# Causal cross attention: the mask products of a batch become a step of their own on TensorE

## The chip, the cores and the metric

The kernel runs on one core of one Trainium2 chip. The time is that of the device, in microseconds (us), from one launch. The kernel before took 1401.39 us (median of 3 runs, 1401.38 to 1406.8).

## The reference

Two decoder layers are computed for `x` of 16 batches x 128 positions x 256 features, each sublayer as `x = x + f(layernorm(x))`: a recurrent mixer, grouped cross attention and a mixture of experts, then windowed self attention, **causal cross attention** and a gated feed-forward. The change is in the causal cross attention alone. What it computes, for each batch:

```
qp = q @ Wq.T                          # q: layernorm(x), 128 x 256;  16 heads of 16 features
k, v = split(latent_kv @ Wkv_expand.T) # latent_kv: 128 x 64
scores = (qh @ kh^T) / sqrt(16)        # per head, 128 x 128
scores = where(tril, scores, finfo.min)
out = softmax(scores) @ vh             # back to 128 x 256
return out @ Wout.T
```

## The kernel before, in words

The kernel is one program of stages, one after the other, each with its own streams for the engines. Stage `cross` handles one batch per step, t = 0 to 15, with two sets of buffers (s = t % 2). `pairs` (line 678) writes steps 0 and 1 out, loops over the pairs of steps 2 to 13, and writes 14 and 15 out. Within an engine the order of instructions is the order of the code; engines meet through semaphores (`wait_ge`; `need` is a wait that is left out where the count is a constant of zero or less).

PSUM has eight banks of 512 columns here. Banks 0 to 3 hold the scores of a batch, one bank per unit u (four heads of 128 columns). Banks 4 and 5 take transpositions, bank 6 the attended values, bank 7 (`PJ`) all projections.

The work of one batch, in the order of its data:

- VectorE normalises the rows (L2851). TensorE turns them (`turn_h`, L2642) and ScalarE copies them out (L2777).
- TensorE projects keys and queries into bank 7 (`project_qk`, L2650 and L2655). ScalarE copies bank 7 to `qk` (L2785).
- GpSimd spreads the keys over a block diagonal of two heads (L2613, two products of 256 columns), and each of the two raises `spread`. After that GpSimd splits pieces of the last stage's weights into a high and a low part (L2625, L2628).
- TensorE projects the values into bank 7 (`project_v`, L2661), once `qk` is copied out. ScalarE copies them (L2789).
- TensorE makes the scores (`scores`). First it writes the additive causal mask into each of the banks 0 to 3, as a product of an identity and the mask in bf16 (L2668, 512 columns, one for each u; 128 rows of the array). Then it adds the products of queries and spread keys (L2673, tiles of 32 rows), eight of them, which the trace counts as 16. A mask product for u must come after VectorE has read that bank for the batch before (`shifted`).
- VectorE takes each row's maximum (L2858) and subtracts it (L2861, which raises `shifted`), for u = 0 to 3. ScalarE takes the exponential (L2794).
- One step later TensorE turns the weights (L2689), ScalarE copies them (L2799), and TensorE multiplies by the values (L2699). ScalarE copies the result (L2804), TensorE turns it (`turn_out`, L2708), and VectorE divides (L2868, L2873). Another step later TensorE turns it again (`turn_out_f`, L2718), ScalarE copies it (L2808), TensorE projects it (L2724), and VectorE adds it to `x` (L2878).

So TensorE's step t (`one`) reads: `scores(t)`, `turn_out_f(t-2)`, `finish_weights(t-1)` with `turn_h(t+1)` in it, `project_qk(t+1)`, `turn_out(t-1)`, `project_v(t+1)`; then `scores(t+1)` begins the next step with its wait for `spread`. The order is written by hand; no planner is involved. VectorE and ScalarE run their own fixed orders, with `shift(t, u)` for u = 0 to 3 first on VectorE. SyncE loads the context of batch t once two batches before it has its values projected (L2597).

The last stage (`silu_ffn`, lines from 2906) starts when the cross stage has ended on all engines.

Of the kernel before, what the change touches and what calls it, by code (L numbers as in the profile page):

```python
# [28 lines left out]
KC = D // P  # L29
# [54 lines left out]
def need(engine, sem, count):  # L84


    if not isinstance(count, int) or count > 0:
        engine.wait_ge(sem, count)  # L88
# [589 lines left out]
def pairs(engine, one, steps=NB):  # L678


    for s in range(2):
        one(s, s, s == 0, False)
    with engine.Fori(1, steps // 2 - 1) as p:
        for s in range(2):
            one(2 * p + s, s, False, False)
    for s in range(2):
        one(steps - 2 + s, s, False, s == 1)
# [1838 lines left out]
def cross(nc, net, sem):  # L2526
# [15 lines left out]
    def number(what, t, u=0):  # L2542

        if what == "h":
            return 0 if isinstance(t, int) and t == 0 else 5 * t - 4
        return 5 * t + 2 + u - (isinstance(t, int) and t == NB - 1)

    def begun(t, n):

        return not (isinstance(t, int) and t < n)  # L2550

    with ExitStack() as ctx:
# [17 lines left out]
        tables_ready = sem("cr_tables")  # L2570
# [7 lines left out]
        spread = sem("cr_spread")  # L2578
# [23 lines left out]
        def _(pool):  # L2602
# [15 lines left out]
            def split_ffn1(t):  # L2618

                piece = bass.ds(t * P, P)  # L2620
                matrices = [[tile.rearrange("p c n -> p (c n)")[:, piece] for tile in of] for of in (
                    (net.gate1_high, net.gate1_low, net.gate1), (net.up1_high, net.up1_low, net.up1),
                    (net.down1_high, net.down1_low, net.down1))]
                for hi, _, w in matrices:
                    own.did(pool.tensor_tensor(hi, w, net.ones[:], ALU.mult))  # L2625
                own.wait()
                for hi, lo, w in matrices:
                    own.did(pool.tensor_tensor(lo, w, hi.bitcast(F32), ALU.subtract))  # L2628
# [5 lines left out]
        def _(pe):  # L2634
            ident = net.const[:, CONST["ident"]]

            def turn_h(t, s):
                pe.wait_ge(normed, t + 1)
                if begun(t, 2):
                    pe.wait_ge(taken, number("p", t - 2, 2) + 1)  # L2640
                for c in range(KC):
                    mm = pe.transpose(ps[:, bank_of("h"), c * P:c * P + P], h_tok[:, s, c * P:c * P + P], ident)  # L2642
                mm.then_inc(turned, 1)

            def project_qk(t, s):
                pe.wait_ge(context_in[s], (t - s) * 8 + 16)
                need(pe, added, t - 2)
                need(pe, proj_taken, 2 * t)
                for oc in range(KC):
                    pe.matmul(ps[:, PJ, D + oc * P:D + oc * P + P], net.xwkv[:, oc * P:oc * P + P],  # L2650
                              context[:, s, :], start=True, stop=True)
                pe.wait_ge(taken, number("h", t) + 1)
                for oc in range(KC):
                    for c in range(KC):
                        mm = pe.matmul(ps[:, PJ, oc * P:oc * P + P], net.xwq[:, c, oc * P:oc * P + P], h_t[:, c, :],  # L2655
                                       start=(c == 0), stop=(c == KC - 1))
                mm.then_inc(projected, 1)

            def project_v(t, s):
                pe.wait_ge(proj_taken, 2 * t + 1)  # L2660
                pe.matmul(ps[:, PJ, 0:D], context[:, s, :], net.xwkv[:, D:2 * D],  # L2661
                          start=True, stop=True).then_inc(projected, 1)

            def scores(t, s):
                pe.wait_ge(spread, KC * (t + 1))
                for u in range(U):
                    need(pe, shifted, U * (t - 1) + u + 1)
                    pe.matmul(ps[:, u, :], ident_b[:], mask.rearrange("p j t -> p (j t)"), start=True, stop=False,  # L2668
                              skip_group_check=True)
                for c in range(KC):  # L2670
                    for u in range(U):
                        g = 32 * u
                        mm = pe.matmul(ps[:, u, c * D:c * D + D], qk[g:g + 32, s, 0, c, :], kbd[g:g + 32, s, c, :, :],  # L2673
                                       start=False, stop=True, skip_group_check=True)
                        if c == KC - 1:
                            mm.then_inc(scored, 1)
# [26 lines left out]
            def turn_out(t):  # L2703
                pe.wait_ge(out_taken, t + 1)

                pe.wait_ge(taken, number("p", t, 3) + 1)
                for u in range(U):
                    mm = pe.transpose(ps[:, bank_of("o"), u * P:u * P + P], out_t[:, u * P:u * P + P], ident)  # L2708
                mm.then_inc(out_turned, 1)

            def turn_out_f(t):
                pe.wait_ge(out_ready, KC * (t + 1))

                pe.wait_ge(proj_taken, 2 * (t + 3) if not (isinstance(t, int) and t >= NB - 2) else 2 * NB)
                if isinstance(t, int) and t >= NB - 2:
                    pe.wait_ge(added, t)
                for c in range(KC):
                    mm = pe.transpose(ps[:, PJ, c * P:c * P + P], out.rearrange("p c u j d -> p c (u j d)")[:, c, :], ident)  # L2718
                mm.then_inc(out_f_turned, 1)
# [7 lines left out]
            def finish_weights(t, s, between=None):  # L2727

                turn_weights(t, s, 0)
                turn_weights(t, s, 1)  # L2730
                if begun(t, 1):
                    project_out(t - 1)
                attend(t, s, 0)
                turn_weights(t, s, 2)
                attend(t, s, 1)
                turn_weights(t, s, 3)
                attend(t, s, 2)
                if between is not None:
                    between()
                attend(t, s, 3)  # L2740

            def one(t, s, first, last):
                scores(t, s)
                if begun(t, 2):
                    turn_out_f(t - 2)
                if first:
                    turn_h(t + 1, 1 - s)
                elif last:
                    finish_weights(t - 1, 1 - s)
                else:  # L2750
                    finish_weights(t - 1, 1 - s, lambda: turn_h(t + 1, 1 - s))
                if not last:
                    project_qk(t + 1, 1 - s)
                if not first:
                    turn_out(t - 1)
                if not last:
                    project_v(t + 1, 1 - s)

            pe.wait_ge(net.in_late, 16 * 6)
            turn_h(0, 0)  # L2760
            project_qk(0, 0)
            project_v(0, 0)
            pe.wait_ge(tables_ready, 2)
            pairs(pe, one)
            t, s = NB - 1, 1
            turn_out_f(t - 1)
# [461 lines left out]
```

## Time and profile before

| | |
|---|---|
| Median of 3 runs | 1401.39 us |
| The profiled execution, its own time | 1413.56 us |
| Span of the profiled execution | 1411.8 us |
| Mean granted clock of TensorE in it | 0.947 of full |
| Busy share of the span: TensorE products, weight loads, VectorE, ScalarE, GpSimd | 87%, 67%, 68%, 54%, 43% |

The span runs from the first to the last instruction. The busy shares are averages over six sublayers that differ; a stage has to be read by itself. The ends of TensorE's instructions are modelled, and neighbours overlap, so distances are best taken from start to start.

### The profile page before, as it was taken

What the parts mean: (1) busy time and instruction counts of PE and PEld (TensorE: products, weight loads), DVE (VectorE), ACT (ScalarE), POOL (GpSimd) and SP (SyncE); (2) the same over time, 40 slices, a digit from 0 to 9 for tenths busy, and PEclk for the clock granted to TensorE, in tenths of its full rate; (3) what the DMA queues carried; (4) which work ended last, traced back from release to release, by engine and by line L of the source; (5) the groups of instructions that cost most, each with busy time, mean ns of one, the idle gap of its engine ahead of it and who ended that gap; (6) DMA issues with size and microseconds to landing.
All of it is one profiled execution on the core that took longest, in us unless ns stands there. A gap on an engine that the chain in (4) does not pass through costs nothing. (4 is left out here: it accounts for less than half of the span.)

```text
span 1411.8 us, 24813 instructions
## 1 busy us (share of the span) xinstructions
PE 1228.2 (87%) x7726; PEld 944.1 (67%) x7726; DVE 958.2 (68%) x1855; ACT 761.3 (54%) x1757; POOL 606.2 (43%) x745
## 2 busy tenths in 40 slices
PE   6894899989989985489999999999977999969998
PEld 4672444478878864367777777777764555648887
DVE  5999899837755358877787778777754666633443
ACT  6442577743545364566666666666643555533332
POOL 2001456452254444776666666666644333320000
PEclk9997899969999998699999999999997999979999
DMA  9001000010035314200000000000000000000000
GB/s 330 1 0 58 10 16 17 9 60 1 23 94 147 98 45 165 108 1 1 2 0 0 0 0 0 0 0 0 1 1 6 3 3 3 2 1 1 15 15 31
DMA packets 27422, 44.74 MB, mean 32 GB/s; under 512 B 5648, under 2 KB 22160, under 8 KB 25936
## 3 DMA queue, kind: packets, MB, share of 16 engines
q1 hardware_dynamic: 23888, 34.31, 7.0%
q0 software_dynamic: 3456, 9.44, 2.5%
q8 instruction: 42, 0.69, 0.2%
q14 instruction: 36, 0.29, 0.1%
HBM read 32.21 MB, written 9.44 MB: 29 GB/s over the span
## 5 line engine op out<-in xcount | busy, mean ns | idle before, releaser
L2334 ACT ACTIVATE wi_weights<-wi_psum,wi_bias,wi_scale 128x128 f32<-128x128 f32 x256 | 113.7, 453 | 120.1 <-DVE wi_bias L2454 120.1
L2109 POOL TENSOR_TENSOR wi_straight<-wi_straight,wi_crossed 128x512 f32<-128x512 f32 x80 | 103.1, 1288 | 10.9 <-DVE wi_crossed L2440 10.8
L978 DVE TENSOR_REDUCE gq_least<-gq_psum 128x4 f32<-128x512 f32 x128 | 84.6, 685 | 15.2 <-PE gq_psum L861 13.5
L2097 POOL TENSOR_TENSOR wi_scratch<-wi_sums,wi_eps 128x4 f32<-128x4 f32 x80 | 33.7, 422 | 129.5 <-DVE wi_sums L2413 128.1
L2098 POOL TENSOR_TENSOR wi_scale<-wi_scratch,minus_half 128x4 f32<-128x4 f32 x80 | 84.6, 1057 | 6.3
L940 ACT ACTIVATE gq_weights_t<-gq_psum 128x512 f32<-128x512 f32 x128 | 67.7, 601 | 23.4 <-PE gq_psum L881 23.2
L2445 DVE TENSOR_REDUCE wi_top<-wi_psum 128x4 f32<-128x512 f32 x64 | 43.8, 685 | 45.8 <-PE wi_psum L2224 45.8
L2175 PEld LDWEIGHTS wi_psum<-const,wi_straight 128*128 128x128 f32 x320 | 39.1, 142 | 53.3 <-issue 34.8
L2858 DVE TENSOR_REDUCE cr_top<-cr_psum 128x4 f32<-128x512 f32 x64 | 43.6, 681 | 45.9 <-PE cr_psum L2673 45.9
L2427 DVE TENSOR_TENSOR wi_straight<-wi_raw,rows 128x512 f32<-128x512 f32 x80 | 71.6, 895 | 0.0
L2233 PE MATMUL wi_psum<-wi_weights_t,wi_values 128*128 128x512 f32 x128 | 68.1, 613 | 2.8 <-DVE wi_weights_t L2461 1.4
L2119 POOL TENSOR_TENSOR wi_weights<-wi_weights,wi_inverse 128x512 f32<-128x512 f32 x64 | 66.4, 1038 | 9.5 <-remote 5.1
L2224 PEld LDWEIGHTS wi_psum<-wi_k_t,wi_q_t 128*128 128x128 f32 x512 | 68.5, 194 | 1.7
L2224 PE MATMUL wi_psum<-wi_k_t,wi_q_t 128*128 128x128 f32 x512 | 68.2, 276 | 0.0
L2613 POOL TENSOR_TENSOR cr_keys_diagonal<-cr_qk,const 128x256 f32<-128x256 f32 x32 | 19.4, 626 | 111.9 <-ACT cr_qk L2785 111.9
L2398 DVE TENSOR_TENSOR wi_out_low<-wi_psum,wi_out_high 128x512 fp32r<-128x512 f32 x64 | 44.0, 687 | 31.7 <-ACT wi_out_high L2341 31.7
L2440 DVE TENSOR_TENSOR wi_crossed<-wi_raw,const 128x256 f32<-128x256 f32 x160 | 65.5, 448 | 0.0
L1247 POOL DMA_INDIRECT ex_slot_rows<-ffn_rows,ex_token x40 | 38.7, 967 | 61.3 <-DVE ex_token L1746 39.4
L2175 PE MATMUL wi_psum<-const,wi_straight 128*128 128x128 f32 x320 | 49.8, 279 | 16.1 <-POOL wi_straight L2109 11.0
L793 POOL TENSOR_TENSOR gq_h_parts<-gq_h_tok,ones 128x512 fp32r<-128x512 f32 x16 | 17.0, 1063 | 108.6 <-DVE gq_h_tok L969 100.7
L3051 DVE TENSOR_TENSOR ff_gated<-ff_gated,ff_psum 128x512 f32<-128x512 f32 x32 | 22.0, 688 | 57.9 <-PE ff_psum L2971 57.6
L861 PE MATMUL gq_psum<-gq_keys_diagonal,gq_h_t 128*128 128x512 f32 x128 | 57.5, 492 | 2.7 <-ACT gq_h_t L930 1.6
(410 smaller groups left out, 3804.5 us busy)
## 6 DMA issues: line engine op xcount, KB each, us to landing
slot_y<-ex_s_out SPq DMA_DIRECT2D x20, 256.0 KB
x<-in_x_dram SPq DMA_DIRECT2D x4, 512.0 KB, 7.9
gate<-in_gate_dram SPq DMA_DIRECT2D x2, 1024.0 KB, 5.6
up<-in_up_dram SPq DMA_DIRECT2D x2, 1024.0 KB, 7.6
down<-in_down_dram SPq DMA_DIRECT2D x2, 1024.0 KB, 9.9
egu<-in_egu_dram SPq DMA_DIRECT2D x1, 2048.0 KB, 14.3
gq_keys_diagonal<-gq_key_parts SPq DMA_DIRECT2D x64, 32.0 KB, 1.9
wo<-in_wo_dram SPq DMA_DIRECT2D x1, 2048.0 KB, 8.8
```

Of the source, the lines that this page charges most:

```text
L861: pe.matmul(ps[:, j % 2, :], h_t[:, n % SLOTS, j * P:j * P + P], kbd[n // 2 % KEYS][:, n % 2, :, :], start=True, stop=True).then_inc(score ...
L940: act.activation(weights_t[:, 4 * (n % 2) + v], ps[:, 2 + v, :], ACT.Exp, scale=-1.0).then_inc(weighed, 1)
L978: dve.tensor_reduce(least[:, n // 2 % 2, n % 2, j, :], ps[:, j % 2, :].rearrange("p (v t) -> p v t", t=P), AX.X, ALU.min).then_inc(topped, 1)
L2098: found = pool.tensor_tensor(scale[:, scale_at], scratch2[:], net.half[:, 0:4], ALU.pow)
L2109: added_up = pool.tensor_tensor(straight[:, at], straight[:, at], crossed[:, at], ALU.add)
L2119: pool.tensor_tensor(weights[:, g % 2], weights[:, g % 2], wide(inverse[:, g % 2], [P, 4, P]), ALU.mult).then_inc(normalised, 1)
L2175: mm = pe.transpose(ps[:, bank_of(what, g), j * P:j * P + P], straight[:, slot(what, g), j, :], ident)
L2224: mm = pe.matmul(bank[:, j * P:j * P + P], q_t[:, g % 2, j, :], k_t[:, s, g, :], start=False, stop=(j == 3), skip_group_check=True)
L2233: pe.matmul(ps[:, AV, :], values[:, s, g * DH:g * DH + DH], weights_t[:, g % 2], start=True, stop=True).then_inc(attended, 1)
L2334: act.activation(weights[:, g % 2, j, :], ps[:, SC + g % 2, j * P:j * P + P], ACT.Exp, bias=bias[:, g % 2, j:j + 1], scale=scale[:, g, j:j ...
L2427: dve.tensor_tensor(straight[:, at], raw[:, at], over_heads(cos[:]), ALU.mult).then_inc(parts, 1)
L2440: dve.tensor_tensor(crossed[:, at, :, to], raw[:, at, :, source], over_heads(sin[:, to]), ALU.mult).then_inc(parts, 1)
```

## The change

The four mask products leave `scores(t)` and become a step `masks(t)`, with their waits for `shifted`. In the step of the batch before, `masks(t + 1)` is called after `turn_out(t - 1)` and ahead of `project_v(t + 1)`. For batch 0 it stands between `project_qk(0)` and `project_v(0)`, and the wait for the two small tables (identity and mask in bf16) moves ahead of it. `scores(t)` keeps the wait for `spread` and the products of queries and keys. No instruction is added or removed, and the order on the other engines stays.

```diff
-            def scores(t, s):
-                pe.wait_ge(spread, KC * (t + 1))
+            def masks(t):
                 for u in range(U):
                     need(pe, shifted, U * (t - 1) + u + 1)
                     pe.matmul(ps[:, u, :], ident_b[:], mask.rearrange("p j t -> p (j t)"), start=True, stop=False,
                               skip_group_check=True)
+
+            def scores(t, s):
+                pe.wait_ge(spread, KC * (t + 1))
                 for c in range(KC):
...
                 if not first:
                     turn_out(t - 1)
                 if not last:
+                    masks(t + 1)
                     project_v(t + 1, 1 - s)
...
             project_qk(0, 0)
+            pe.wait_ge(tables_ready, 2)
+            masks(0)
             project_v(0, 0)
-            pe.wait_ge(tables_ready, 2)
             pairs(pe, one)
```

## Rows read from the trace of the kernel before

**Rows 1.** The table of stretches: busy us of each engine, granted clock, DMA share, GB/s.
```profile
core 0: us, PE busy (x) PEld busy (x) DVE busy (x) ACT busy (x) POOL busy (x), PEclk, DMA share, GB/s
1095.00:1239.00 144.00, 130.00 (x1213) 85.16 (x1212) 92.14 (x180) 83.16 (x167) 48.47 (x104) 1.00 0.01 3
```

**Rows 2.** The waits from 1084 to 1239 us: total us, times, longest.
```profile
POOL cr_keys_diagonal L2613 <- ACT cr_qk L2785: 103.4, 14, 7.7
...
PE cr_psum L2668 <- POOL cr_keys_diagonal L2613: 10.5, 14, 0.8
...
PE cr_psum L2661 <- ACT cr_qk L2785: 4.0, 14, 0.3
```

**Rows 3.** Instructions in order of time, one step: start, us, engine, line, operation.
```profile
1155.52 0.69 DVE L2861 TENSOR_TENSOR cr_weights<-cr_psum,cr_top 128x512 f32<-128x512 f32 x1
...
1156.31 0.60 PE L2708 MATMUL cr_psum<-const,cr_out_t 128*128 128x128 f32 x4
1156.51 0.60 ACT L2785 ACTIVATE cr_qk<-cr_psum 128x512 f32<-128x512 f32 x1 [0.45 <-PE cr_psum L2655]
...
1157.16 0.70 PE L2661 MATMUL cr_psum<-xwkv,cr_context 64*128 64x256 f32 x2 [0.25 <-ACT cr_qk L2785]
...
1157.28 1.18 POOL L2613 TENSOR_TENSOR cr_keys_diagonal<-cr_qk,const 128x256 f32<-128x256 f32 x2 [7.37 <-ACT cr_qk L2785]
...
1158.61 1.03 PE L2668 MATMUL cr_psum<-cr_mask,cr_ident 128*128 128x512 bf16 x4 [0.75 <-POOL cr_keys_diagonal L2613]
...
1159.57 1.15 PE L2673 MATMUL cr_psum<-cr_keys_diagonal,cr_qk 32*128 32x256 f32 x16
...
1160.65 0.46 POOL L2628 TENSOR_TENSOR down_low<-down,down_high  x1
1160.65 0.44 PE L2718 MATMUL cr_psum<-const,cr_out 128*128 128x128 f32 x2
1160.74 0.69 DVE L2858 TENSOR_REDUCE cr_top<-cr_psum 128x4 f32<-128x512 f32 x1 [2.12 <-PE cr_psum L2673]
```

**Rows 4.** Single instructions of that step: the last three transpositions, the last mask.
```profile
1156.42 0.49 PE L2708 MATMUL cr_psum<-const,cr_out_t 128*128 128x128 f32 x3
...
1159.27 0.38 PE L2668 MATMUL cr_psum<-cr_mask,cr_ident 128*128 128x512 bf16 x1
```

**Rows 5.** Durations by line, ns min/median/max: L2661, then the first four of L2673.
```profile
L2661 PE MATMUL cr_psum<-xwkv,cr_context x26: 376/428/480, 1089.9 to 1224.8; 64*128 64x256 f32 x26
...
L2673 PE MATMUL cr_psum<-cr_keys_diagonal,cr_qk x4: 478/478/478, 1159.6 to 1159.6; 32*128 32x256 f32 x4
```

**Rows 6.** Instructions in order of time: the step before the one of rows 3.
```profile
1146.09 1.23 POOL L2613 TENSOR_TENSOR cr_keys_diagonal<-cr_qk,const 128x256 f32<-128x256 f32 x2 [7.41 <-ACT cr_qk L2785]
...
1147.45 1.03 PE L2668 MATMUL cr_psum<-cr_mask,cr_ident 128*128 128x512 bf16 x4 [0.79 <-POOL cr_keys_diagonal L2613]
...
1148.42 1.15 PE L2673 MATMUL cr_psum<-cr_keys_diagonal,cr_qk 32*128 32x256 f32 x16
```

**Rows 7.** TensorE in order of time: batches 0 and 1.
```profile
1066.70 1.22 PE L2661 MATMUL cr_psum<-xwkv,cr_context 64*128 64x256 f32 x2 [0.69 <-ACT cr_qk L2785]
1068.12 1.86 PE L2668 MATMUL cr_psum<-cr_mask,cr_ident 128*128 128x512 bf16 x4 [0.21 <-POOL cr_keys_diagonal L2613]
1069.92 2.09 PE L2673 MATMUL cr_psum<-cr_keys_diagonal,cr_qk 32*128 32x256 f32 x16
...
1075.75 2.08 PE L2655 MATMUL cr_psum<-cr_h_t,xwq 128*128 128x128 f32 x8 [2.64 <-ACT cr_h_t L2777]
1078.51 1.22 PE L2661 MATMUL cr_psum<-xwkv,cr_context 64*128 64x256 f32 x2 [0.69 <-ACT cr_qk L2785]
1079.78 1.89 PE L2668 MATMUL cr_psum<-cr_mask,cr_ident 128*128 128x512 bf16 x4
1081.60 1.53 PE L2673 MATMUL cr_psum<-cr_keys_diagonal,cr_qk 32*128 32x256 f32 x16
```

**Rows 8.** Stretches of the table with a lower clock: cross's start, its end.
```profile
1062.00:1072.00 10.00, 8.91 (x37) 5.21 (x37) 1.53 (x4) 1.36 (x3) 7.82 (x12) 0.50 0.03 9
...
1246.50:1250.00 3.50, 3.41 (x14) 3.08 (x14) 0.04 (x1) 1.58 (x3) 0.00 (x0) 0.55 0.02 5
```

**Rows 9.** Durations, ns min/median/max: VectorE's normalisation, all 16.
```profile
L2851 DVE TENSOR_SCALAR cr_h_tok<-x,mean_var,rstd x16: 403/435/1007, 1061.6 to 1224.9; 128x256 f32 x12, 128x256 f32<-128x256 f32 x4
```

**Rows 10.** Groups by line, windowed stage: busy us, mean ns, idle before.
```profile
L2398 DVE TENSOR_TENSOR wi_out_low<-wi_psum,wi_out_high 128x512 fp32r<-128x512 f32 x64 | 44.0, 687 | 31.7 <-ACT wi_out_high L2341 31.7
```

## The prediction

> **What bounds the kernel now.** I read the page's shares first. They are averages over unlike stages, so the next view is the table of stretches for the cross stage alone. There TensorE is busy 130.0 of 144 us, at full clock, and no other engine is above 92.1 [rows 1]. TensorE sets the pace of the stage, and what it loses in each step are waits. The view of waits names two that matter: 10.5 us for the spread keys, in front of the masks, and 4.0 us for the copied `qk`, in front of the values' projection. Each comes 14 times, once per batch [rows 2]. GpSimd's own 103.4 us of waiting [rows 2] shows that it is not short of time: it sits until `qk` arrives.
>
> One step in order of time shows why [rows 3]. The projection of keys and queries ends. ScalarE copies `qk` (1156.51 to 1157.11), GpSimd spreads the keys (1157.28 to 1158.46), and the masks start at 1158.61, 0.15 after it. Beside that chain of about 2.2 us TensorE has only the four transpositions (from 1156.31) and the values' projection (from 1157.16). It then spends 1158.61 to 1159.57 on masks, which need neither `qk` nor the keys. Only at 1159.57 come the products that do. VectorE waits until 1160.74, so it and everything behind it follow the scores.
>
> **The change, part by part.** Nothing is removed or added; four products per batch change place on one queue.
>
> *Masks out of the way of the scores.* From the first mask to the first score is 1159.57 - 1158.61 = 0.96 us [rows 3], and 1148.42 - 1147.45 = 0.97 in the step before [rows 6]; the steps alternate between these two forms. If the scores may start where the masks start now, each batch gains 0.96.
>
> *Do they fit into the gap?* I lay out the new order from start to start. The last transposition starts at 1156.42 + 0.49 - 0.27 = 1156.64: three of them last 0.49 and one 0.27 (0.49 less two steps of 0.11) [rows 4]. The masks start at 1156.75. They stream every 0.22, and from the last mask (1159.27) to the first score (1159.57) is 0.30 [rows 3, 4]; so a group of masks and the change to tiles of fewer rows take 0.96 together. The values' projection then starts at 1157.71. `qk` was copied out at 1157.11, so its wait is gone. Its two products: the first lasts up to 480 ns after a stop, the other 376 [rows 5]; with 0.70 for both, the second starts 0.70 - 0.376 = 0.32 later. It streams 0.22, and I allow 0.09 for the change of tile as at the masks: scores could start at 1157.71 + 0.32 + 0.31 = 1158.34. The keys let them start at 1158.61. TensorE has 0.27 to spare, so the keys decide. In the other form (transpositions from 1145.04, same layout, keys 0.13 before 1147.45) the spare is about 0.38 [rows 6].
>
> *First score after a stop.* Now the first four score products stand behind the masks and still last 478 ns against 374 for the rest, so they already pay for an exposed weight load [rows 5]. I charge nothing more. What the trace doesn't show is a score group right behind a 64-row product. From below it costs no more than the change from the masks (0.08, in my layout); from above I take that the scores start only when the modelled end of the projection has passed, 1157.71 + 0.70 = 1158.41, still 0.20 inside. I take the former; neither touches the sum at full clock.
>
> The Trainium skill, TensorEngine Tiling (Array Packing), section Tiling Modes, says that changing the tiling mode drains TensorE. The row agrees in kind: 0.30 against 0.22 from the last mask. Here the changes per batch go from three (to 64 rows, back to 128, to 32) to two (to 64, to 32); by that rule with a full drain behind each the sum would be 0.2 us smaller, all of it in batches 0 and 1.
>
> *The moved wait for `shifted`.* The masks of t+1 now wait, early, for VectorE's subtraction of u = 3 of batch t, and behind them in the queue stand the projection, ScalarE's copy of the values, and the scores. That subtraction ends at 1155.52 + 0.69 = 1156.21; the masks come at 1156.75, 0.54 later [rows 3]. Both hang on the scores' start, so the cover stays when the step shrinks. Past it and the spare of 0.27, each us of a late VectorE costs one us. I cost it at nothing.
>
> *What is later.* The projection of values starts about 0.55 later (1157.71 for 1157.16). ScalarE copies it after its exponential of u = 3, then waits for bank 7 at 1161.12 less 0.96; the copy (0.38) ends near 1158.8. SyncE's next context load slips by as much, and its context is used more than a step later. GpSimd's weight splitting ends at 1161.11 [rows 3], and now runs beside VectorE's first maximum and subtraction, which start near 1159.78. The nearest row for that is L2398 of the windowed stage, the same shape from PSUM and SBUF: 687 ns in the mean [rows 10], against 0.69 here; no cost. From above, VectorE's normalisation, which does fall beside GpSimd's work, goes from 403 to 1007 ns [rows 9]; I keep that for the rival.
>
> *Batches 2 to 15:* 14 x 0.96 = 13.5 us.
>
> *Batches 0 and 1* run at the 1.2 GHz level (granted 0.50) [rows 8]. There masks take 1069.92 - 1068.12 = 1.80 and the projection up to 1.27 (1078.51 to 1079.78, with no wait behind it), so TensorE and not the keys decides, and the gain is the idle time that is filled. In batch 1 the projection of queries ends at 1077.83 and streams on some 0.18 before its modelled end, so the next product could start at 1077.65; the values start at 1078.51 [rows 7]. That is 0.86, less 0.08 for one change of tile that was hidden in the wait: 0.8. Batch 0 has the same and 0.15 held by the keys (1.42 from projection to masks against 1.27) [rows 7]: 0.9. The bounds are the rows' idle times (0.69 + 0.69 + 0.21 = 1.6) and half a mask group each more (3.4). I take 1.7.
>
> **Sum:** 13.5 + 1.7 = 15.2 us. Profiled execution: 1413.56 - 15.2 = 1398.4. It was 12.2 us above the median of the runs, which I put down to nothing in this stage. Median: 1401.4 - 15.2 = 1386.2. All of it passes to the end, because the last stage starts when this one has ended.
>
> **The rivals.**
>
> *The clock moves (0.15).* TensorE is busier from 1066 to 1082, so its clock may rise earlier. At full clock the scores of batch 0 take 1.15 instead of 2.09 and the masks of batch 1 1.03 instead of 1.89 [rows 3, 7]: 1.8 us more, 1384.4. The reverse is a lower clock in other stretches near the stage's end: one such stretch holds 3.4 us of work at 0.55 [rows 8], and another like it costs about 1.6, 1387.8. For it speaks only that these stretches move against the rest.
>
> *TensorE becomes the bound before the scores (0.09).* If the unseen change from 64 to 32 rows costs 0.3 us more than the spare, the gain is 0.66 x 14 + 1.7 = 10.9 and the time 1390.5. Against it: changes of tile cost 0.08 where a row shows them [rows 4].
>
> *The gain goes nowhere (0.05).* If the scores were held by something after the keys, the time stays at 1401.4. Against it: the masks start 0.15 after GpSimd ends, and the score products follow without a stop [rows 3].
>
> *The early wait holds the queue: slower (0.02).* Place: the masks' wait for u = 3. If GpSimd's splitting stretches VectorE's first maximum and subtraction as it did the normalisation (x 2.5), `shifted` is 0.69 x 1.5 x 2 = 2.06 late. Less 0.54 cover and 0.27 spare that is 1.25 per batch against 0.96 gained: 14 x 0.29 = 4.1, less 1.7, so 1403.8. It decides from a delay of 0.54 + 0.27 + 0.96 = 1.77. Rows 10 speak against it.
>
> **How the numbers follow.** The forecast (1385 to 1388) has 0.69. The range takes in the clock case and the TensorE-bound one and the bounds of the first two batches: 1383 to 1391.5. A measurement of this kernel can tell about 0.5%, 7 us, from no change. Faster by more than that is under 1394.4: the first three cases, 0.93. Within it: 0.06, the cases of no gain and nearly all of the slower one. Slower: 0.01.
>
> **What would show it.** Right: in a step at full clock the order is L2708, L2668, L2661, L2673, the scores' idle time is 0.2 to 0.4 us until L2613, no wait stands in front of L2661 or L2668, and a step is 10.25 us where it was 11.2. Wrong: a wait of L2668 for L2861; no wait of L2673 for L2613 (TensorE bounds); L2858 or L2861 longer than 0.7 beside GpSimd; a step that shrank by less than 0.9; or batches 0 and 1 off their 1.7 because the clock rose at another time.

## The result: medians of 1401.64 and 1384.72 us, a ratio of 0.9864, more gained than forecast

| | before | after |
|---|---|---|
| Median (4 runs each) | 1401.64 us (1401.38 to 1406.8) | 1384.72 us (1384.03 to 1385.64) |
| Ratio, 95% interval | | 0.9864 (0.9843 to 0.9886) |
| Span of the profiled execution | 1411.8 us | 1382.5 us |
| Cross stage, start of the first transposition to start of the last addition to `x` | 196.3 us | 178.4 us |

The medians differ by 16.9 us, and the ratio says 19 us (16 to 22); forecast were 15.2. The median of after lies inside the forecast range, 0.9864 of the time before (1382.6) just below its lower end of 1383. The two profiled executions differ by 29.3 us, but 11.9 of these lie ahead of the cross stage, where nothing was changed: its first transposition starts at 1062.2 in the one and at 1050.3 in the other.

In the changed kernel the mask products are L2667, the scores L2675, and lines behind them are 2 or 4 higher. One step, in order of time (start, us, engine, line, operation), beside [rows 3]:

```profile
1136.09 0.69 DVE L2865 TENSOR_TENSOR cr_weights<-cr_psum,cr_top 128x512 f32<-128x512 f32 x1
...
1136.89 0.60 PE L2710 MATMUL cr_psum<-const,cr_out_t 128*128 128x128 f32 x4
1137.09 0.60 ACT L2789 ACTIVATE cr_qk<-cr_psum 128x512 f32<-128x512 f32 x1 [0.45 <-PE cr_psum L2655]
1137.22 0.64 PEld L2667 LDWEIGHTS cr_psum<-cr_mask,cr_ident 128*128 128x128 bf16 x4
...
1137.54 0.81 PE L2667 MATMUL cr_psum<-cr_mask,cr_ident 128*128 128x512 bf16 x3
...
1137.86 1.18 POOL L2613 TENSOR_TENSOR cr_keys_diagonal<-cr_qk,const 128x256 f32<-128x256 f32 x2 [6.32 <-ACT cr_qk L2789]
...
1138.28 0.70 PE L2661 MATMUL cr_psum<-xwkv,cr_context 64*128 64x256 f32 x2
...
1139.09 0.74 PEld L2675 LDWEIGHTS cr_psum<-cr_keys_diagonal,cr_qk 32*128 32x128 f32 x16 [0.52 <-POOL cr_keys_diagonal L2613]
1139.09 1.15 PE L2675 MATMUL cr_psum<-cr_keys_diagonal,cr_qk 32*128 32x256 f32 x16
...
1140.26 0.69 DVE L2862 TENSOR_REDUCE cr_top<-cr_psum 128x4 f32<-128x512 f32 x1 [1.07 <-PE cr_psum L2675]
```

The order is the forecast one: transpositions (L2710), masks (L2667), values (L2661), scores (L2675). (The record of the first mask product is missing; its weight load is there.) From the transpositions to the scores it took 1159.57 - 1156.31 = 3.26 us [rows 3] and takes 1139.09 - 1136.89 = 2.20. The projection of values no longer waits, the masks wait for nothing (the subtraction ends at 1136.78, some 0.5 ahead of them), and the scores start 0.05 after GpSimd ends at 1139.04. In the table of stretches the steady part now reads, beside [rows 1]:

```profile
1079.00:1209.00 130.00, 126.59 (x1198) 85.33 (x1204) 93.04 (x180) 83.51 (x168) 46.98 (x101) 1.00 0.01 3
```

TensorE is busy 97% of it, where it was 90%. In the waits from 1085 to 1200 us, the ones in front of TensorE's values and masks are gone, and this is left in front of the scores:

```profile
PEld cr_psum L2675 <- POOL cr_keys_diagonal L2613: 6.5, 11, 0.6
...
PE cr_psum L2675 <- POOL cr_keys_diagonal L2613: 1.5, 6, 0.2
```

### The profile page after: what moved, and what is told of

Same layout as the page of the kernel before. It is cut to its first block and busy times, and to the rows that moved or that the text cites. A ratio compares the mean times of both kernels' runs of the same rounds, so it can differ in the third digit from the quotient of the medians.

```text
span 1382.5 us, 24786 instructions
## 1 busy us (share of the span) xinstructions
PE 1214.4 (88%) x7679; PEld 940.9 (68%) x7726; DVE 957.8 (69%) x1855; ACT 760.1 (55%) x1757; POOL 606.2 (44%) x745
## 5 line engine op out<-in xcount | busy, mean ns | idle before, releaser
L2224 PEld LDWEIGHTS wi_psum<-wi_k_t,wi_q_t 128*128 128x128 f32 x512 | 68.4, 194 | 1.7
```

The costliest lines, as they stand in the source:

```text
L2224: mm = pe.matmul(bank[:, j * P:j * P + P], q_t[:, g % 2, j, :], k_t[:, s, g, :], start=False, stop=(j == 3), skip_group_check=True)
```

## The experiments

Two theories have to be kept apart. A: the place of the masks on TensorE's queue gives a fixed amount per batch, as long as the keys and not TensorE set the start of the scores. B: the rest of the difference between the first two traces is TensorE's clock, which falls to its 1.2 GHz level in other places in every execution. C came up while the traces were read: a wait whose count is held in a register costs time when it stands behind the wait that matters.

All traces, cut at the start of the scores of batches 0, 1, 2 and 15 (s0, s1, s2, s15), in us. The stage goes from the start of its first transposition to the start of its last addition to `x`:

```
                      stage  to s0  s0-s1  s1-s2  s2-s15 (a batch)  after s15   stage starts at
before                196.3  7.72   11.68  10.70  145.42 (11.186)   20.75       1062.2
e5  before            196.3  7.72   11.69  10.71  145.44 (11.188)   20.75       1050.5
e10 before            196.4  7.72   11.61  10.86  145.42 (11.186)   20.75       1050.4
e12 before            196.3  7.69   11.56  10.92  145.42 (11.186)   20.75       1050.0
after                 178.4  6.44   10.69  10.66  131.94 (10.149)   18.63       1050.3
e1  after             179.1  6.49   10.69   9.26  131.94 (10.149)   20.68       1050.2
e11 after             179.1  6.60   10.54   9.26  131.94 (10.149)   20.75       1055.3
e2  waits hoisted     195.0  7.72   11.74  10.64  144.71 (11.131)   20.21       1051.0
e3  split wait        175.8  6.60   10.60   9.07  128.79 ( 9.907)   20.76       1052.5
e4  values first      183.2  7.53   11.50  10.09  134.80 (10.369)   19.32       1049.2
e6  one extra mask    175.4  6.84    8.00   9.29  132.23 (10.172)   19.09       1049.8
e7  four extra masks  186.9  7.65    9.97   9.93  139.98 (10.768)   19.32       1050.8
e8  masks too early   208.1  6.60   13.26  11.74  156.57 (12.044)   19.95       1050.2
e9  split and extra   179.3  6.94   10.79   9.29  131.57 (10.121)   20.73       1049.4
```

The column from s2 to s15 repeats to 0.02 us in four traces of the kernel before and to 0.01 in three of the changed one. It is the yardstick for everything that follows.

**The changed kernel again (e1, 5 runs; e11, one run).** No edit.

> The changed kernel again, to have a second trace of it. Theory A (place of the masks): scores to scores takes 10.15 us a batch from batch 2 to 15, as in the first trace (11.19 before), and this is the same in every execution; the gain over the kernel before is 13.5 us there and about 2.3 in batches 0 and 1. Theory B (clock): the parts of the cross stage that the first trace shows beyond this (2.1 us less after the last scores, 1.0 us more between the scores of batches 1 and 2) are stretches at the 1.2 GHz level that fall elsewhere by chance; they differ in this trace by up to 2 us. Rival: they come from the order and repeat to 0.2 us. Time: 1384 to 1386 us.

> The changed kernel, a third trace. 10.15 us a batch. Theory B: the time between the scores of batches 1 and 2 (10.66 and 9.26 so far) and after the last scores (18.65 and 20.66) fall again among such values, with no fixed pair.

Measured for e1: 1384.5 us (1380.26 to 1387.03), ratio 0.9854 (0.9828 to 0.988); for e11: 1389.62 in one run. The step is 10.149 us in both, as in the first trace. The parts around it move: s1 to s2 took 10.66, 9.26 and 9.26 us in the three traces, and the time after s15 18.63, 20.68 and 20.75. The rows say that it is the clock. After s15, in the first trace of the changed kernel:

```profile
1218.93 0.44 PE L2720 MATMUL cr_psum<-const,cr_out 128*128 128x128 f32 x2 [0.87 <-DVE cr_out L2877]
1219.20 1.04 PE L2691 MATMUL cr_psum<-const,cr_weights 128*128 128x128 f32 x8
1220.08 1.03 PE L2726 MATMUL cr_psum<-xwout,cr_out_f 128*128 128x256 f32 x4
```

and in e1:

```profile
1217.42 0.61 PE L2720 MATMUL cr_psum<-const,cr_out 128*128 128x128 f32 x2 [0.87 <-DVE cr_out L2877]
1217.82 1.91 PE L2691 MATMUL cr_psum<-const,cr_weights 128*128 128x128 f32 x8
1219.53 1.74 PE L2726 MATMUL cr_psum<-xwout,cr_out_f 128*128 128x256 f32 x4
```

The same instructions of the same program, with the same waits ahead of them, last 1.04 and 1.91 us. For these stretches of the changed kernel B holds.

**The kernel before again (e5, 12 runs; e10 and e12, one run each).** No edit.

> The kernel before again, for a second trace of it. Theory B (clock): the 12 us by which its first profiled execution was above the median lie ahead of the cross stage and are not there again, and the stretches at the 1.2 GHz level at the end of the cross stage (2.1 us more than in the changed kernel) and after batch 1 differ from its first trace. Rival: both repeat. Scores to scores 11.19 us a batch in any case. Time 1401.4 us.

> The kernel before, a third trace. The steps from scores to scores are 11.19 us a batch. Theory B (clock by chance): the time after the last scores (20.8 and 20.7 us in two traces, 18.7 and 20.7 in two of the changed kernel) or the one between the scores of batches 1 and 2 is off by 1 to 2 us in some of the three traces of each kernel, and so is some stage ahead of the cross stage in an execution near 1407. Rival: the kernel before always has 20.7 to 20.8 after the last scores.

> The kernel before, a fourth trace, for the same question: 11.19 us a batch, and the 5.5 us between its two groups of times (near 1401.5 and near 1407) lie ahead of the cross stage, not in it. Rival: they lie in the cross stage.

Measured: e5 1402.48 us (1401.31 to 1407.46), e10 1401.93, e12 1401.41. The 11.9 us ahead of the stage were not there again. They arose between 290 and 500 us, in the mixture of experts: the first trace is 1.3 us ahead of e5's when it enters this stretch and 12.1 us behind it at the end. The granted clock from 290 to 400 us and from 400 to 500 was 0.87 and 0.95 there, and 0.91 and 1.00 in e5. An estimate from these shares gives the clock at most 110 x 0.04 + 100 x 0.05, some 9 of the 13.4 us. So B holds for a part of this difference only, and no cause is shown for the rest. The stage itself took the same in both.

The time after s15 was 20.75 in all four traces of the kernel before: B's expectation that it would vary there too missed, and the rival to it holds. That stretch was at the low clock in every trace of the kernel before, and in two of three of the changed one. s1 to s2 moved by 0.2 only.

The times of the kernel before fall into two groups. Of 50 runs (the first 4, 34 measured beside e1 to e8, and e5's 12), 24 lie between 1400.8 and 1402.7 and 23 between 1406.0 and 1407.7. None of the traces fell on one near 1407, so e12's question, where in the program the difference lies, has no answer from the kernel before itself. That it goes with the clock can be read from the runs: in the 46 of them whose mean granted clock is on record, it is 0.948 to 0.952 in the lower group and 0.946 or 0.947 in the upper. The span times one less this mean is the most that the lower level can have cost. It comes to 70.8 and 75.4 us in the mean of the two groups, 4.6 of the 5.2 us between them. For the changed kernel, e11 at 1389.62 us (clock 0.945) started its cross stage at 1055.3, 5.1 us later than e1 at 1384.5 (clock 0.949), and the stage itself took the same: that difference lies ahead of the stage.

**The waits alone, in the kernel before (e2, 12 runs).** The masks stay behind the wait for the keys.

```diff
             def scores(t, s):
+                need(pe, shifted, U * t)
                 pe.wait_ge(spread, KC * (t + 1))
                 for u in range(U):
-                    need(pe, shifted, U * (t - 1) + u + 1)
                     pe.matmul(ps[:, u, :], ident_b[:], ...
```

> The kernel before, with the masks where they were, behind the wait for spread keys; only the four waits for the subtractions of the batch before (counts held in registers inside the loop) are one wait now and stand ahead of the wait for the keys. Theory C: in the kernel before, the evaluation of these counts stands between the end of GpSimd's spreading and the first mask (0.13 and 0.15 us there, 0.05 before the first score in the changed kernel). Then the first mask starts 0.05 us after GpSimd ends, each of the 14 looped and late batches gains 0.08 to 0.10 us, 1.2 us in all, 1400.2 us. Rival: the 0.1 us belongs to a bf16 mask product after a stop; then nothing changes: 1401.4 us and still 0.13 to 0.15.

Measured: 1403.42 us (1399.75 to 1409.8), where 1400.2 was expected; ratio 0.9992 (0.9974 to 1.0009). The time can't resolve an effect of this size; the trace can. In the kernel before, within the loop and then in the written-out step 15 (GpSimd's spreading, then the first weight load of the masks):

```profile
1157.28 1.18 POOL L2613 TENSOR_TENSOR cr_keys_diagonal<-cr_qk,const 128x256 f32<-128x256 f32 x2 [7.37 <-ACT cr_qk L2785]
...
1158.60 0.55 PEld L2668 LDWEIGHTS cr_psum<-cr_mask,cr_ident 128*128 128x128 bf16 x4 [1.15 <-issue]
...
1235.51 1.18 POOL L2613 TENSOR_TENSOR cr_keys_diagonal<-cr_qk,const 128x256 f32<-128x256 f32 x2 [7.12 <-ACT cr_qk L2785]
...
1236.74 0.55 PEld L2668 LDWEIGHTS cr_psum<-cr_mask,cr_ident 128*128 128x128 bf16 x4 [0.97 <-POOL cr_keys_diagonal L2613]
```

and in e2, within the loop:

```profile
1145.73 1.18 POOL L2613 TENSOR_TENSOR cr_keys_diagonal<-cr_qk,const 128x256 f32<-128x256 f32 x2 [7.29 <-ACT cr_qk L2785]
...
1146.96 0.55 PEld L2668 LDWEIGHTS cr_psum<-cr_mask,cr_ident 128*128 128x128 bf16 x4 [1.07 <-POOL cr_keys_diagonal L2613]
```

From GpSimd's end to the weight load it is 0.14 us in the loop of the kernel before, where the counts of the waits in between are held in registers, 0.05 in its step 15, where they are constants, and 0.05 in e2's loop, where they stand ahead. The releaser changes too: "issue" in the first, GpSimd in the other two. The rival as it was put (a bf16 product after a stop, so that nothing changes) falls. But e2's steps 14 and 15, which are written out, went the other way, though no count is in a register there. Step 15 in e2:

```profile
1223.56 1.18 POOL L2613 TENSOR_TENSOR cr_keys_diagonal<-cr_qk,const 128x256 f32<-128x256 f32 x2 [7.18 <-ACT cr_qk L2785]
...
1224.86 0.56 PEld L2668 LDWEIGHTS cr_psum<-cr_mask,cr_ident 128*128 128x128 bf16 x4 [1.03 <-issue]
```

GpSimd ends at 1224.74, and the weight load comes 0.11 later instead of 0.05. It is 0.12 for batch 0 in both traces too, where the wait for the keys is the only one in front of the masks. So with constants the gap is 0.05 when another, long met, wait stands behind the one for the keys, and 0.11 or 0.12 when none does. The scores of the changed kernel, fp32 products with the keys' wait alone in front of them, start 0.05 after GpSimd in the loop and in steps 14 and 15, so the product may matter too. Which waits stand where changes the gap by up to 0.09 us; that the register is the cause is not shown, and e2 also made one wait of four.

With this the step closes. In the loop the two forms of the step fell from 11.27 and 11.16 to 11.20 and 11.07 us, and the last two steps rose by 0.08 each: 11 x 0.08 - 2 x 0.08 = 0.72 us less over the 13 batches, or 0.055 in the mean, as in the table.

**Masks behind the values (e4, 6 runs).** Half of the change: ahead of the wait for the keys, but not filling the time in which ScalarE copies.

```diff
-                    masks(t + 1)
                     project_v(t + 1, 1 - s)
+                    masks(t + 1)
...
-            masks(0)
             project_v(0, 0)
+            masks(0)
```

> The changed kernel with the masks behind the projection of values, still ahead of the wait for the keys. This undoes half of the change. Theory A: the projection waits for the copied queries and keys again (0.25 to 0.33 us), the masks then end 0.2 to 0.25 us after the keys are there, so TensorE bounds: 10.35 to 10.4 us a batch against 10.15, 3 us in 14 batches, and 0.8 us more in each of batches 0 and 1: 1389 us. Rival: only being ahead of the wait for the keys counts, the order within does not: 1384.7 us.

Measured: 1388.94 us (1387.25 to 1395.77), ratio 0.9912 (0.9886 to 0.9937), 10.369 us a batch. Both are what A expects. In its trace the values wait again, GpSimd is done at 1140.34, and the scores start 0.29 later, because TensorE is still at the masks:

```profile
1139.04 0.70 PE L2661 MATMUL cr_psum<-xwkv,cr_context 64*128 64x256 f32 x2 [0.25 <-ACT cr_qk L2789]
1139.16 1.18 POOL L2613 TENSOR_TENSOR cr_keys_diagonal<-cr_qk,const 128x256 f32<-128x256 f32 x2 [6.50 <-ACT cr_qk L2789]
...
1139.89 0.81 PE L2667 MATMUL cr_psum<-cr_mask,cr_ident 128*128 128x512 bf16 x3 [0.16 <-issue]
1140.63 1.15 PE L2675 MATMUL cr_psum<-cr_keys_diagonal,cr_qk 32*128 32x256 f32 x16
```

So of 1.04 us a batch, 0.82 come from being ahead of the wait for the keys and 0.22 from being ahead of the values.

**The spare time, filled (e6, 5 runs; e7, 6 runs).** One, or all four, of the mask products of a batch issued twice; `start=True` makes the second write the same.

```diff
-                    pe.matmul(ps[:, u, :], ident_b[:], mask...
+                    for _ in range(2 if u < 1 else 1):      # e7: u < 4
+                        pe.matmul(ps[:, u, :], ident_b[:], mask...
```

> The changed kernel with the first mask product of each batch issued twice: 0.22 us more TensorE work per batch at the full clock, 0.43 at the lower one. Theory A: in the changed kernel the keys bound the scores and TensorE has 0.2 to 0.35 us to spare, so from batch 2 on this is hidden but for at most 0.04 us a batch; batches 0 and 1 pay 0.43 each: 0.9 to 1.4 us in all, 1385.6 to 1386.1 us. Rival (TensorE bounds): 14 x 0.22 + 0.9 = 4 us, 1388.7 us.

> The changed kernel with every mask product issued twice: 0.86 us more per batch at the full clock. Theory A: the spare is used up and the rest shows, 0.86 less 0.2 to 0.35 is 0.5 to 0.65 us a batch, 7 to 9 us in 14 batches, and 1.7 in each of batches 0 and 1: 1395 to 1397 us. Rival: no spare, 12 + 3.4 us, 1400 us.

Measured: e6 1385.71 us (1380.47 to 1388.19), 10.172 a batch: 0.22 us of work costs 0.023. e7 1394.21 us (1392.53 to 1399.49), 10.768 a batch: 0.86 costs 0.62, so 0.24 were free. Its step is as A expects, its time 0.8 us under the expected range. The changed kernel has about 0.24 us of TensorE time to spare per batch in the mean, and the keys set its pace.

**The wait for the keys split (e3, 5 runs; e9, one run).** If the keys bound, letting the first half of the scores start on the first half of the keys should free that spare.

```diff
             def scores(t, s):
-                pe.wait_ge(spread, KC * (t + 1))
                 for c in range(KC):
+                    pe.wait_ge(spread, KC * t + c + 1)
```

> The changed kernel, where the scores of the first half (c = 0) wait for the first of GpSimd's two spreading products alone, and those of the second half for the second. Theory A, with the keys as the bound of the changed kernel and TensorE 0.2 to 0.35 us behind: scores start that much earlier, 0.2 to 0.3 us a batch, 2.5 to 4 us in all: 1381 to 1382.5 us. Rival 1: TensorE itself was the bound: no change, 1384.7. Rival 2: the second wait between the products costs 0.1 us or more a batch: 1383 or above.

> The kernel with the split wait for the keys, and the first mask product of each batch issued twice, one look. Theory A: with the wait split TensorE itself is the bound (9.91 us a batch), so the 0.22 us that was all but free in the changed kernel (10.15 to 10.17) now shows in full: 10.1 to 10.15 us a batch. Rival: 9.93, the product is still hidden and the keys or another engine set the pace.

Measured: e3 1382.09 us (1378.45 to 1383.47), ratio 0.9835 (0.9813 to 0.9857), 9.907 a batch, 0.24 less than the changed kernel. It beats both kernels in the trace; by the times its interval overlaps e1's. In e3 TensorE is busy 118.87 of 120 us:

```profile
1137.25 1.18 POOL L2613 TENSOR_TENSOR cr_keys_diagonal<-cr_qk,const 128x256 f32<-128x256 f32 x2 [6.00 <-ACT cr_qk L2789]
1137.67 0.70 PE L2661 MATMUL cr_psum<-xwkv,cr_context 64*128 64x256 f32 x2
...
1138.29 1.15 PE L2675 MATMUL cr_psum<-cr_keys_diagonal,cr_qk 32*128 32x256 f32 x16
```

The scores start 0.62 after the values, 0.14 before GpSimd is done with the second half. e9 adds e6's extra product to it, and now 0.22 us of work cost 10.121 - 9.907 = 0.21. The same product is free in one kernel and paid in full in the other: with the split wait, TensorE bounds.

**Masks earlier still (e8, 6 runs).** The forecast's slower rival, made to happen by the place of the masks and not, as there, by a slower VectorE.

```diff
                 if not last:
+                    masks(t + 1)
                     project_qk(t + 1, 1 - s)
...
-                    masks(t + 1)
                     project_v(t + 1, 1 - s)
```

> The changed kernel with the masks of the next batch ahead of the projection of keys and queries. The fourth mask then has to wait for VectorE's last subtraction (7.8 us after the start of the scores, where that projection starts 6.25 after it), and the projection stands behind it. Theory A: the projection starts at 8.15 instead of 6.25, and nothing fills the gap behind it: 12.0 us a batch, where the kernel before has 11.2 and the changed one 10.15; slower than before by 10 us: 1408 to 1412 us. Rival (the early wait costs nothing, because the subtraction is in time): 11.1 us a batch, 1400 us.

Measured: 1414.18 us (1412.75 to 1417.66), ratio 1.0074 (1.0051 to 1.0097), 12.044 a batch: slower than the kernel before. The time is 2 us above the expected range (s0 to s1 took 13.26), and the step is as expected.

```profile
1161.41 0.69 DVE L2865 TENSOR_TENSOR cr_weights<-cr_psum,cr_top 128x512 f32<-128x512 f32 x1
1162.16 0.39 PE L2667 MATMUL cr_psum<-cr_mask,cr_ident 128*128 128x512 bf16 x1 [0.79 <-DVE cr_weights L2865]
1162.48 0.71 PE L2650 MATMUL cr_psum<-cr_context,xwkv 64*128 64x128 f32 x4
...
1165.16 1.23 POOL L2613 TENSOR_TENSOR cr_keys_diagonal<-cr_qk,const 128x256 f32<-128x256 f32 x2 [8.27 <-ACT cr_qk L2789]
1166.45 1.15 PE L2675 MATMUL cr_psum<-cr_keys_diagonal,cr_qk 32*128 32x256 f32 x16 [0.71 <-POOL cr_keys_diagonal L2613]
```

The fourth mask waits 0.79 us for the subtraction that ends at 1162.10, the projection of keys stands behind it, and the gap that the masks used to fill is idle again.

## Why the mechanism was right, and which steps of the sum failed

Two terms of the sum were too small. "Batches 2 to 15: 14 x 0.96" measured 1.037 a batch, and the 1.7 us for batches 0 and 1 measured 2.1 to 2.3. With them the sum is 16.8 us where it was 15.2, and the traces show 17.2 to 18.0 us for the stage. A third step failed in a smaller way: the clock was left out of the sum, as a rival with 0.15. The paragraphs below take these one by one, after what was right.

**What bounds, and the mechanism: right.** The scores followed the masks, which waited for something they did not need. The signs came: the order, no wait in front of values or masks, and the scores waiting for GpSimd. Their idle time was put at 0.2 to 0.4 us and is 0.12 and 0.24 in the two forms of the step. The step shrank to 10.15, forecast 10.25.

**Fit into the gap: right.** The layout put the values 0.96 behind the first mask and the scores, were the keys there, 0.63 behind the values. The values start 1.39 behind the transpositions (forecast 1.40), and e3, where the keys don't hold them, starts its scores 0.62 behind the values. In the changed kernel they start 0.81 and 0.94 behind them, so the spare is 0.19 and 0.32. It was put at 0.27 and 0.38, and e7 measured 0.24 in the mean.

**The drain between tiling modes: too strong here.** Scores behind the values start 0.62 later in e3, before the modelled end of the projection at 0.70; in batch 1 of the changed kernel, at the lower clock, they start 1.15 behind (1066.30 to 1067.45), modelled end 1.22. What the Trainium skill, TensorEngine Tiling (Array Packing), section Tiling Modes, calls a drain costs at most the 0.09 of the layout here, not a wait for that end. By that rule the prediction made the gain of batches 0 and 1 0.2 us smaller; it came out 0.4 to 0.6 larger than the 1.7.

**"Batches 2 to 15: 14 x 0.96": the step that was mis-sized.** It measured 1.037 a batch from s2 to s15. The forecast let the scores start where the masks had started, 0.13 to 0.15 after GpSimd. They start 0.05 after it. Over these 13 batches the parts close: 13 x 0.965 = 12.55 for the masks, and 0.085 for each of the 11 steps in the loop (0.94), make 13.49; measured were 13.48. That the kernel before pays this in its loop and not in steps 14 and 15 could be read from its own trace.

**Batches 0 and 1: 1.7 forecast, 2.1 to 2.3 measured.** Batch 0 gained 1.09 to 1.28 and batch 1 0.87 to 1.15. The cost of the values in front of the next product was taken as 1.27, "with no wait behind it", from batch 1. That was wrong: GpSimd ends at 1079.72 there and the weights load at 1079.77, so the keys held it. Without a wait it is 1.15.

**The early wait for `shifted`, and GpSimd beside VectorE: right at no cost.** VectorE's first maximum and subtraction last 0.69 each beside GpSimd's splitting, and the fourth subtraction ends some 0.5 us ahead of the masks. The 1007 ns of [rows 9], on which the rival rested, are one normalisation (at 1065.16 us), and what GpSimd did beside it was setting the value buffers (L2605, L2607), not splitting. Beside the splitting (L2625) the normalisation does stretch, in every other step from 0.43 to 0.63 us in both kernels, but the maximum and the subtraction do not. e8 shows the price once that cover is gone.

**The clock: a rival that partly came in.** The stage takes 196.3 or 196.4 us in the traces of before and 178.4, 179.1 and 179.1 in those of after: 17.2 to 18.0 us. The forecast plus the two corrections above is 15.2 + 14 x 0.077 + 0.5 = 16.8. The rest is the clock. In e1 and e11 it rises earlier: the products of scores 1 take 1.15 us, where they took 1.53 [rows 7], and s1 to s2 shrinks by 1.4 to 1.7, where 1.04 is the masks' part. In the first trace of the changed kernel it rises later (these products take 2.09), which takes back the 1.0 of batch 2, but there it did not fall in the stretch after s15, which gave 2.1.

**What stays open.** The ratio says 19 us, the stage shows 17.2 to 18.0, inside the ratio's interval. The changed kernel's 9 runs of the first measurement and e1 have a mean of 1384.1, the 50 of the kernel before 1404.2. That is 20.1, some 2.5 more than the stage shows. By the granted clocks of these runs (0.9506 and, in the 46 on record, 0.9480 in the mean) the lower level can have cost 68.4 us in the one and 73.0 in the other, so the clock is enough to fill this. Where in the program it differs, and whether by chance of the draw or by the change, is not shown: no trace of the kernel before near 1407 exists.

## What to carry to other kernels

Work that needs nothing from a slow chain belongs ahead of the wait for it, in the gap that the chain leaves, and the layout from start to start says whether it fits: here 0.96 us of masks fitted with 0.24 to spare. Moved too far, the same work meets its own wait and holds the queue. When a wait is the last thing on the path, look also at which waits stand between it and the first instruction behind it: here they moved the start by up to 0.09 us.

## What was unexpected of the hardware

- On TensorE, the time from the end of GpSimd's last spreading product to the first weight load of the masks depended on the waits in between: 0.12 to 0.14 us in the loop of the kernel before (counts in registers, the subtractions' wait behind the keys'), 0.05 in e2's loop (the subtractions' wait ahead), and with constants 0.05 in the first order and 0.11 in the second. In the view of waits the longer ones appear as "issue". Which part of a wait costs this is open.
- Where the clock rises was worth more than a product. e6 has one product per batch more than the changed kernel, and its clock rose during the values of batch 0: the products of scores 0 took 1.15 us instead of 2.09, and s0 to s1 8.00 us instead of 10.7. That was one trace, and it does not show that the extra product was the reason: the changed kernel itself has runs at 1380.3 us with a granted clock of 0.953, as short as e6's 1380.47 at 0.954.
